# Query path of a two-layer cross-attention kernel: turns by DMA instead of TensorE, scale and bias by ScalarE and GpSimd, matrix integers by GpSimd

## What is computed

```
def _qdq(x):
    s = maximum(max(abs(x), axis=-1) / 127, 1e-8)
    return clip(round(x / s), -127, 127) * s
q = _qdq(x) @ _qdq(wq).T + bq
```

## Time and profile before

| | us |
|---|---|
| runs | 962.68, 962.88, 965.32 (median 962.88) |
| the profiled execution's own time | 966.35 |
| its span, first to last instruction | 964.6 |
| TensorE busy | 821.9 |
| VectorE busy | 759.5 |
| ScalarE busy | 576.9 |
| GpSimd busy | 487.2 |

### The profile page before, as it was taken

The page is one execution under the profiler, slowest core; times in us unless marked ns, Lnnn a source line. Parts: engine busy times, 40 slices in busy tenths (PEclk is TensorE's granted clock), DMA queues, the critical chain, the costliest instruction groups (busy, mean ns, idle before and its releaser), DMA issues.

```text
span 964.6 us, 14534 instructions
## 1 busy us (share of the span) xinstructions
PE 821.9 (85%) x4373; PEld 353.2 (37%) x4373; DVE 759.5 (79%) x1510; ACT 576.9 (60%) x974; POOL 487.2 (51%) x560
## 2 busy tenths in 40 slices
PE   2899987789898989899999968799999999974754
PEld 2544443334344444444444432222223232222321
DVE  4699998879899899999998758477777777634884
ACT  3588886543555565666665544466666666655762
POOL 2866663223334444444444343475757575764761
PEclk9999999899999999999999986899999999996886
DMA  8668875533353442352433241212122221000111
GB/s 283 214 178 221 223 204 151 143 88 65 62 115 55 72 103 57 63 70 55 79 65 65 45 100 54 84 49 79 55 77 57 72 61 46 1 1 0 43 66 66
DMA packets 172392, 86.51 MB, mean 90 GB/s; under 512 B 124048, under 2 KB 156960, under 8 KB 172320
## 3 DMA queue, kind: packets, MB, share of 16 engines
q1 hardware_dynamic: 172320, 85.64, 35.6%
HBM read 37.76 MB, written 12.58 MB: 52 GB/s over the span
## 4 chain that ended last, share of the span: by engine, by line
PE 37%; DVE 22%; issue 7%; ACT 6%; SPq 4%; DMA 3%; POOL 0%; ACTq 0%; DVEq 0%
PE bank L1098 10%; PE bank L1190 5%; PE bank L1161 5%; PE bank L1110 4%; PE bank L1180 4%; DMA A<-B 3%; DVE bank L1516 3%; DVE gsm L1518 3%; DVE B L1527 2%; SPq L438 2%; DVE B L1521 2%; PE bank L1307 2%; ACT bank L806 2%; PE bank L1209 2%; PE bank L1199 2%
## 5 line engine op out<-in xcount | busy, mean ns | idle before, releaser
L1098 PE MATMUL bank<-A,B 128*128 128x512 f16 x1024 | 233.0, 381 | 15.8 <-DVE B L1527 15.6
L1642 DVE TENSOR_REDUCE B<-bank 128x1 f32<-128x512 f32 x256 | 168.0, 683 | 73.9 <-PE bank L1161 73.9
L936 ACT ACTIVATE A<-bank 128x512 f32<-128x512 f32 x256 | 144.1, 593 | 106.9 <-PE bank L1180 103.5
L594 POOL TENSOR_TENSOR B<-B 128x512 f16<-128x512 f32 x64 | 76.4, 1193 | 223.4 <-DVE B L1527 147.2
L1098 PEld LDWEIGHTS bank<-A,B 128*128 128x128 f16 x1024 | 98.8, 98 | 142.9 <-DVE B L1527 20.6
L663 POOL TENSOR_TENSOR B<-A 128x512 f32<-128x512 f32 x64 | 79.3, 1269 | 96.0 <-ACT A L936 96.0
L806 ACT ACTIVATE bank<-B 128x512 f32<-128x512 f32 x64 | 38.5, 602 | 137.4 <-DVE B L1521 137.4
L1110 PE MATMUL bank<-A,B 128*128 128x512 f16 x512 | 120.7, 379 | 0.0
L1180 PE MATMUL bank<-A 98*128 98x512 f16 x256 | 94.5, 390 | 21.2 <-ACT A L936 10.5
L1161 PE MATMUL bank<-A 96*128 96x512 f16 x256 | 97.7, 409 | 7.9 <-DMA A<-B 4.7
L663 POOL TENSOR_TENSOR B<-B,A 128x512 f32<-128x512 f32 x64 | 79.0, 1264 | 0.1
(11 more groups left out here) (216 smaller groups left out, 1479.5 us busy)
## 6 DMA issues: line engine op xcount, KB each, us to landing
B<-in_L_ffn_w_dram SPq DMA_DIRECT2D x48, 256.0 KB, 3.4
A<-k_parts SPq DMA_DIRECT2D x48, 128.0 KB, 2.6
A<-B SPq DMA_DIRECT2D x192, 32.0 KB, 1.9
X<-in_x_dram SPq DMA_DIRECT2D x4, 1024.0 KB, 9.4
B<-in_ctx_dram SPq DMA_DIRECT2D x16, 256.0 KB, 4.4
k_parts<-B SPq DMA_DIRECT2D x16, 256.0 KB, 4.3
v_rows<-B SPq DMA_DIRECT2D x16, 256.0 KB, 2.3
B<-v_rows SPq DMA_DIRECT2D x16, 256.0 KB, 3.4
```

The source lines that it names most:

```text
L594: nc.gpsimd.tensor_tensor(HLb[j][:, 1, :], Db[j % 2], HLb[j][:, 0, :], ALU.subtract).then_inc(lo_done, 1)
L936: nc.scalar.activation(PR[(HG * t + j) % 8], bank[2 + j % 2][:, :], ACT.Exp, scale=SCALE).then_inc(exp_done, 1)
L1098: last = mm(bank[2 * n + q][:, :], XQT[a][:, m, :], wt[:, m % DB, j * 512:j * 512 + 512], start=(m == 0), stop=(m == 2 * DB - 1))
L1642: reduce(NMX[g % 2][:, t, j:j + 1], bank[ROW_BANKS[r % 3]][:, :], AX.X, ALU.max, negate=True).then_inc(row_max, 1)
```

## The change

- The integers LI of a tile are turned by a DMA of SyncE (`turn_ints`) into LT; `q_diag`, `q_turn` and `q_operands` are gone.
- `q_project` takes the tokens as the stationary side: four matmuls of 512 columns, with tokens in the partitions of the result. It moves from chunk 0 of a tile to chunk 3 of the tile before.
- The token's scale is then one per partition: `q_scale` on ScalarE, in chunk 0. Channel scale and bias are rows spread over all partitions: `q_affine`, two GpSimd instructions on 128x512, in chunk 0. `q_high` (ScalarE) casts, in chunk 2, `q_low` (GpSimd) subtracts, in chunk 3, and `turn_q`, a DMA of SyncE, turns both parts into QALL. `q_full` and `q_bias` are gone.
- `ints_block` goes from VectorE to GpSimd, with two block buffers instead of four.
- The scales of wq go to memory and back in a row over all partitions in tiles 2 and 3, as those of wp did before; these come back behind the loads of attention.
- The product that sums the last matrix and the scale made from it come one and two chunks earlier. L1428 takes its constant from memory instead of from the instruction.
- Behind the stage the orders on all engines are written anew.

```diff
-        SXB, DIAG = part(P, F32), part(P, F32)
-        QF, QB = part(D, F32, "p (k t) -> p k t", k=DB), part(D, F32, "p (k t) -> p k t", k=DB)
+        QF = part(D, F32)
+        QHL_1 = part(2 * D, F16, "p (h d) -> p h d", h=2)
...
-        wm_ints = B[:, used[0]:used[0] + DB * D].rearrange("p (k d) -> p k d", k=DB)
-        OT, SM = part(512, F32), part(512, F32)
...
-                    sp.wait_ge(q_hi, b * TB + TB)
-                    sp.wait_ge(q_lo, b * TB + TB)
+                    for n in range(2):
+                        sp.wait_ge(qT_in[n], 16 * TB // 2 * (b + 1))
...
-                sp.dma_start_transpose((WQT, WLT, WPT)[m][:, :, k * P:k * P + P], wm_ints[:, k, :]).then_inc(wm_out, 16)
+                sp.dma_start_transpose((WQT, WLT, WPT)[m][:, :, k * P:k * P + P],
+                                       wm_ints[k % 2]).then_inc(wm_out, 16)
+
+            def turn_ints(u):
+
+                sp.wait_ge(li3, u + 1)
+                up_to(sp, qp_ps, u)
+                sp.dma_start_transpose(LT, LI).then_inc(lt_in, 16)
+
+            def turn_q(u):
+
+                sp.wait_ge(q_hi, u + 1)
+                sp.wait_ge(q_lo, u + 1)
+                sp.dma_start_transpose(QALL[:, :, :, u * P:u * P + P].rearrange("p h k s -> p (h k) s"),
+                                       QHL[u % 2].rearrange("p h d -> p (h d)")).then_inc(qT_in[u % 2], 16)
...
+            sp.wait_ge(val_sb, DB * BATCH)
+            sp.dma_start(bv_all[:, :], on_all(bq, D)).then_inc(wide_in, 16)
...
+                    if (i, j) == (SCALED[0] + 1, 1):
+                        scales_out(0, 0)
+                    if (i, j) == (SCALED[0] + 2, 1):
+                        scales_in(0)
...
+                    if j == 0 and i > 4:
+                        turn_q(i - 5)
+                    if j == 1 and i > 2:
+                        turn_ints(i - 3)
                     if j == 0 and i < TOK - 1:
                         turn_x(i + 1, (i + 1) % 2)
             sp.wait_ge(b_ps, FC * TOK)
+            turn_ints(TOK - 3)
+            turn_q(TOK - 5)
             for g in range(2):
                 load_kv(0, g, True)
                 load_q(0, g)
+            for i in (TOK - 2, TOK - 1):
+                turn_ints(i)
+                turn_q(i - 2)
             send_c(0, 0)
+            turn_q(TOK - 2)
             for g in range(2, DB):
                 load_kv(0, g, True)
                 load_q(0, g)
+            turn_q(TOK - 1)
+            sp.wait_ge(qb_ready, TOK)
+            scales_in(1)
...
-            nc.gpsimd.memset(eps[:, 4:8], 1e-6)
+            nc.gpsimd.memset(eps[:, 4:8], XUP)
...
-            def q_diag(u):
-                pool.wait_ge(qs3, u + 1)
-                up_to(pool, sx_ps, u)
-                nc.gpsimd.tensor_tensor(DIAG, id32[:, :], QSC[:, 0:1].to_broadcast([P, P]), ALU.mult).then_inc(diag3, 1)
+            def q_affine(u):
+
+                pool.wait_ge(qf_ready, u + 1)
+                if u == 0:
+                    pool.wait_ge(swp_io, 32)
+                    pool.wait_ge(wide_in, 16 * 4)
+                step.link(nc.gpsimd.tensor_tensor(QF, QF, swp_all[:, :], ALU.mult))
+                nc.gpsimd.tensor_tensor(QF, QF, bv_all[:, :], ALU.add).then_inc(qb_ready, 1)
 
             def q_low(u):
                 pool.wait_ge(q_hi, u + 1)
-                nc.gpsimd.tensor_tensor(held[:, 0:1], held[:, 1:2], held[:, 1:2], ALU.add)
-                cols = bass.ds(u * P, P)
-                nc.gpsimd.tensor_tensor(QALL[:, 1, :, cols], QB, QALL[:, 0, :, cols], ALU.subtract).then_inc(q_lo, 1)
+                nc.gpsimd.tensor_tensor(QHL[u % 2][:, 1, :], QF, QHL[u % 2][:, 0, :], ALU.subtract).then_inc(q_lo, 1)
+
+            def ints_block(m, k):
+
+                n = DB * m + k
+                pool.wait_ge(wm_round, ROUNDED(m, k))
+                up_to(pool, wm_out, 16 * n)
+                raw, ints = wm_raw[:, k, :], wm_ints[k % 2]
+                if m != 1:
+                    nc.gpsimd.tensor_scalar(ints, raw, RND, 127.0, ALU.subtract, ALU.min).then_inc(wm_ready, 1)
+                else:
+                    step.link(nc.gpsimd.tensor_scalar(raw, raw, RND, -1.0, ALU.subtract, ALU.max))
+                    nc.gpsimd.tensor_scalar(ints, raw, 1.0, None, ALU.min).then_inc(wm_ready, 1)
...
-                        if j == 0 and there(i - 3):
-                            q_diag(i - 3)
+                        if j == 0 and there(i - 4):
+                            q_affine(i - 4)
...
-                        if j == 2 and there(i - 4):
+                        if j == 3 and there(i - 4):
                             q_low(i - 4)
                         lo_part(i, j)
+                        for m, b in matrix_work(i, j, INTS):
+                            ints_block(m, b)
...
-            q_diag(TOK - 3)
             q_rstd(TOK - 2)
+            q_affine(TOK - 4)
+            q_rstd(TOK - 1)
             q_low(TOK - 4)
-            q_diag(TOK - 2)
-            q_rstd(TOK - 1)
-            q_diag(TOK - 1)
             ones_under(0)
             for u in (TOK - 3, TOK - 2, TOK - 1):
+                q_affine(u)
                 q_low(u)
                 ones_under(u - TOK + 4)
...
-            def q_operands(u):
-                act.wait_ge(sx_ps, u + 1)
-                up_to(act, qp_ps, u)
-                up_to(act, qf_ready, u)
-                nc.scalar.copy(LT.rearrange("p k t -> p (k t)"), bank16[4][:, 0:D])
-                nc.scalar.copy(SXB, bank[4][:, D // 2:D // 2 + P]).then_inc(lt_out, 1)
-
-            def q_bias(u):
-                act.wait_ge(qf_ready, u + 1)
+            def q_scale(u):
+
+                act.wait_ge(qp_ps, u + 1)
                 up_to(act, q_lo, u)
-                for k in range(DB):
-                    last_ = nc.scalar.activation(QB[:, k, :], QF[:, k, :], ACT.Identity, bias=BQ[:, k:k + 1],
-                                                 scale=SWQP[:, k:k + 1])
-                last_.then_inc(qb_ready, 1)
+                nc.scalar.activation(QF, bank[7][:, :], ACT.Copy, scale=QSC[:, u % 4:u % 4 + 1]).then_inc(qf_ready, 1)
+
+            def q_high(u):
                 act.wait_ge(qb_ready, u + 1)
-                nc.scalar.copy(QALL[:, 0, :, bass.ds(u * P, P)], QB).then_inc(q_hi, 1)
+                up_to(act, qT_in[u % 2], 16 * (u // 2))
+                nc.scalar.copy(QHL[u % 2][:, 0, :], QF).then_inc(q_hi, 1)
...
-                        if j == 1 and there(i - 4):
-                            q_bias(i - 4)
+                        if j == 0 and there(i - 4):
+                            q_scale(i - 4)
+                        if j == 2 and there(i - 4):
+                            q_high(i - 4)
...
-            q_bias(TOK - 4)
+            q_scale(TOK - 4)
             q_norm(TOK - 2)
-            q_operands(TOK - 3)
+            q_high(TOK - 4)
             q_round(TOK - 2)
             q_norm(TOK - 1)
-            q_operands(TOK - 2)
+            q_scale(TOK - 3)
             q_round(TOK - 1)
-            q_bias(TOK - 3)
-            q_operands(TOK - 1)
-            q_bias(TOK - 2)
-            q_bias(TOK - 1)
+            q_high(TOK - 3)
+            q_scale(TOK - 2)
+            q_high(TOK - 2)
+            q_scale(TOK - 1)
...
+                if isinstance(n, int) and n == 0:
+                    act.wait_ge(qT_in[0], 16 * TOK // 2)
...
+            q_high(TOK - 1)
...
-            def q_turn(u):
-
-                pe.wait_ge(li3, u + 1)
-                up_to(pe, lt_out, u)
-                for k in range(DB):
-                    turn(bank16[4][:, k * P:k * P + P], LI[:, k * P:k * P + P], id16[:, :])
-                pe.wait_ge(diag3, u + 1)
-                mm(bank[4][:, D // 2:D // 2 + P], ones[:, :], DIAG, start=True, stop=True).then_inc(sx_ps, 1)
-
             def q_project(u):
-                pe.wait_ge(lt_out, u + 1)
+
+                pe.wait_ge(lt_in, 16 * (u + 1))
                 up_to(pe, qf_ready, u)
                 if u == 0:
                     pe.wait_ge(wm_out, 16 * DB)
                 if u == 1:
                     pe.wait_ge(wm_scale, 2)
                 for k in range(DB):
-                    for j in range(DB):
-                        last_ = mm(bank[7][:, k * P:k * P + P], WQT[:, j, k * P:k * P + P], LT[:, j, :],
-                                   start=(j == 0), stop=(j == DB - 1))
+                    last_ = mm(bank[7][:, :], LT[:, k, :], WQT[:, k, :], start=(k == 0), stop=(k == DB - 1))
                 last_.then_inc(qp_ps, 1)
...
-                        if j == 0 and there(i - 4):
-                            q_project(i - 4)
-                        if j == 2 and there(i - 3):
-                            q_turn(i - 3)
-                        if (i, j) == (SUMMED_AT + 1, 2):
+                        if j == 3 and there(i - 3):
+                            q_project(i - 3)
+                        if (i, j) == (SUMMED_AT + 1, 1):
...
-            q_project(TOK - 4)
             down(TOK - 1, 0, 1)
```

(25 more changed lines are left out.)

68 lines of the change are left out of this document (33 added, 35 removed).

## The result

The changed kernel takes 1012.85 us (median of 4, 1011.01 to 1013.51), against 964.1 us before in the same session: a ratio of 1.050 (95% interval 1.047 to 1.053). Slower was the likeliest case of the prediction, but 974.5 us was the forecast and 990 the end of its range: of 48.8 us lost the forecast had 11.6. That the kernel would get slower was forecast, but mostly not for the reason that it did: the way into attention, which the forecast had, is under a third of the loss. The profiled execution took 1012.25 us around a span of 1010.3; the span of before was 964.6, and the 45.7 us between the two spans are what the traces have to account for.

A forecast was written before the change was run, and what follows sets the result against it. VectorE was taken to set the stage's pace, TensorE meeting it towards tile 14, and SyncE's queue the way into attention. -9 + 7 + 13.6 = +11.6 on 962.88 gave 974.5 us; range 960 to 990.

The forecast's parts named there:

- the DMA turn of LI: Feed-forward stage: the turn lands before `q_project` while VectorE is less than 0.5 us behind; cost nothing.
- Matrix integers, -9: Matrix tiles: VectorE sheds 16.5 us, contention with GpSimd returns 2.2, 2.2 and 3.2; -9 us, with 1.2 us instructions.
- my phases: Matrix tiles: GpSimd's new instructions delay VectorE by about 0.9, 0, 0.7 and 0.65 us in a matrix's four chunks.
- `q_full` away and `q_affine` added, +7: Tiles from 4 on: VectorE loses 0.72 us a tile but waits for GpSimd; +7 us, bounds -3 and +12.
- the forecast's VectorE tile: Steady tiles of the stage: VectorE needs 21.9 to 22.2 us a tile against 21.5 before.
- Into attention, +13.6: Between stage and attention: SyncE's queue order delays the first score of group 1 by 13.6 us, bounds 11 and 16.
- The stand at `q_project(14)`: Into attention: TensorE idle about 9 us between third and fourth score block, until the DMA of LT lands.
- (a): Into attention: SyncE issues `turn_ints(13)` and `turn_q(11)` ahead of the first keys; +2.6 us.
- (b): Into attention: `turn_ints(14)` goes out behind 24 query DMAs, holding back score blocks and maxima; +10.4 us, (a) included.
- (c): Into attention: `turn_q(14)`, `turn_q(15)` and `scales_in` stand ahead of sending group 1's maxima; +3.2 us.
- Behind it, nothing: After the first score of group 1: TensorE and ScalarE set a fixed pace, so no further gain or loss.
- Rival 1: Matrix tiles: GpSimd's `tensor_scalar` goes by columns, 2.6 us each, giving +11 instead of -9; 994 us, chance 0.24.

The follow-up runs named there:

- experiment 4: The kernel before with `ints_block` alone moved to GpSimd, old query path and four block buffers kept: 954.19 us, ratio 0.989.
- experiment 10: Changed kernel with `q_project` one chunk later, SyncE reordered inside and between stages, GpSimd's block wait loosened, no 4-byte writes in the stage: 958.93 us, ratio 0.994.
- experiment 9: Changed kernel without 4-byte writes in the stage: first scale row made by TensorE and ScalarE, second written during attention: 999.3 us, ratio 1.036.
- Experiment 5: Changed kernel with only SyncE's order between the stages redone, moving `turn_ints`, `turn_q` and `scales_in` of the last tiles: 1003.04 us, ratio 1.039.
- experiment 11: The kernel of experiment 4 with the load of group 3 moved behind the maxima of group 1 in SyncE's list: 955.04 us, ratio 0.990.
- experiment 3: Changed kernel with `ints_block` moved back to VectorE, new query path and two block buffers kept: 1008.07 us, ratio 1.047.

## Why the prediction was wrong

**The step that failed** is the one on the DMA turn of LI: "Hidden while VectorE is less than 0.5 us behind; cover gone, it costs TensorE the difference, which it has to spare. Cost nothing." By the runs it cost the +30.4 us of the stage, and with them the 11.7 us by which the integers alone shorten it (experiment 4: 346.9 us from the first chunk to the last, before 358.6): 42 in all; experiment 10, with the same work, has a stage of 345.3. Three things in it were wrong.

- *The place in the list.* I took the 2.5 us to landing of the earlier trace rows, from a turn with nothing ahead, for all sixteen. The landing held for fourteen; the wait ahead of the issue had no term. What stands ahead on SyncE in tiles 3, 5, 6, 8 and 9 was in the diff and in the code: a 1 MB load, four turns that wait for GpSimd, a write in 4-byte pieces. I priced such a row of issues between the stages, step by step, and not inside the stage. The trace of before had `turn_x` at 6.2 us behind a matrix load, and I didn't ask which turns land late there and don't hurt. The two new transfers of the first scale row had no term either, and the two writes and that read cost 12.3 us of the stage (experiment 9).
- *The slack.* TensorE's 10.4 us held. But "less than 0.5 us behind" was a condition that I didn't check: in the trace of before VectorE starts chunk 1 of tiles 9 to 13 between 4.9 and 0.7 us behind the end of `up`. In the changed kernel it was 1.25 behind in tile 11, and TensorE stood 1.28.
- *What a stand costs.* TensorE had nothing to spare. While it stands, VectorE runs out of work, and both lose the whole time. And it comes back slower: behind the 7.67 us stand of tile 9 the next 28 matmuls took 7.95 us (the row counts the start of a 29th), where 28 of the 0.216 us of a steady tile are 6.05. The windows of the last 6.19 us of the stand and of what follows it, after:

```profile
441.86:448.05 6.19, 0.01 (x1) 0.01 (x1) 4.76 (x11) 0.60 (x1) 1.17 (x2) 0.73 0.31 54
448.05:456.00 7.95, 7.95 (x29) 3.28 (x30) 0.01 (x1) 1.73 (x4) 0.41 (x1) 0.78 0.01 2
```

**Matrix integers, -9.** Right in size where they are alone, -10.3 in experiment 4, but by luck: the instruction is 1.92 us and not 1.2, so something else must make up for it. I take it that a long GpSimd instruction delays VectorE less often than my phases said; that isn't shown. In the changed kernel the gain is not there.

**`q_full` away and `q_affine` added, +7.** Wrong in sign where it can be seen with cover: experiment 10's stage is 1.6 us shorter than experiment 4's. Its steady tiles are 21.73 us, not 21.9 to 22.2, and its tile 14 is 19.8 instead of 21.6: there TensorE sets the pace in experiment 4, and has less to do in experiment 10. The contention is there and of the forecast kind (L1475's mean 849 ns for 719, L1467 no faster), but with cover it is worth 0.2 us a tile. The tiles of 23.0 us in the changed kernel are not the forecast's VectorE tile: they are contention and missing cover together, the 1.3 us at `q_project`.

**Into attention, +13.6.** Right: +14.6. The stand at `q_project(14)` was put at about 9 us and was 9.44; (a) and (b) together were 10.4 and measured 11.7, (c) 3.2 and 2.9. Experiment 5 confirms it from the other side, by undoing (b) and (c).

**Behind it, nothing.** It was +2.1 us, as much as one instruction grew. VectorE's L1744 takes 0.69 us in seven of eight executions, and once this (timeline after):

```profile
954.21 2.41 POOL L738 TENSOR_TENSOR B<-B,swp_all 128x1024 f32<-128x1024 f32 x1
954.33 2.83 DVE L1744 TENSOR_SCALAR B<-B 128x1024 f16<-128x1024 f32 x1
```

It started 0.12 us behind a GpSimd instruction of 2.41 us. The same pair meets in every trace that has both halves of the change (2.83 or 2.84 us), and not in before's, nor in those of experiments 4 and 11 with the old query path, nor in that of experiment 3, which has the new query path and the integers on VectorE. The Trainium skill, "Perfetto Trace Analysis", Optimizing Scalar/DVE Operations, says that GpSimd and VectorE share a read port of SBUF; the rows agree. Why the phase falls this way with both halves was not tried.

**Rival 1** (994 us, instructions by columns) was nearest to the time and is not what happened: by experiment 4 the integers gain. The range left out the case in which a stand of TensorE repeats inside the stage, and it had none for it.

**What stays open:** why the integers on GpSimd bring nothing beside the new query path as it was changed (experiment 3 against the changed kernel) is argued from the turns of blocks that wait for GpSimd in tiles 5, 6 and 8, and not shown by a run of its own; another place for `q_affine` was not tried.
